# A fused two-layer transformer kernel: paired maxima, DMA-transposed keys, PSUM operands, and another way to round the FFN's integers

## What is computed

```python
# layer 0, cross-attention, 16 heads of 8; ctx has 120 positions
q = rms_norm((x @ Wq + bq) per head, gq);  k = rms_norm((ctx @ Wk + bk) per head, gk)
out = softmax(q k^T / sqrt(8)) @ v;        x = x + out @ Wproj + bproj
# layer 0, FFN with integers: act_quant rounds to -128..127 per row, weight_quant to -1, 0, 1
h = act_quant(ln(x)) @ weight_quant(w1)^T; h = silu(depthwise_conv1d(h, 3 taps))
x = x + act_quant(h) @ weight_quant(w2)^T
# layer 1, cross-attention, one head of 128, keys and values are ctx itself
a = softmax((ln(x) @ w1_w^T + w1_b) ctx^T / sqrt(128)) @ ctx
x = x + concat(ln(x), a) @ w2_w^T + w2_b
# layer 1, mixture of 8 experts of width 256, every row goes to all of them
x = x + sum_e softmax(ln(x) @ gate)_e * ((silu(ln(x) @ Wg_e) * (ln(x) @ Wu_e)) @ Wd_e)
```

## Time and profile before

| | |
|---|---|
| median of the runs | 1234.42 us |
| the profiled execution | 1234.41 us, span 1232.5 us |
| TensorE products busy | 1122.8 us (91%), 10033 records |
| VectorE | 1043.8 us (85%), 2728 |
| ScalarE | 836.8 us (68%), 1685 |
| GpSimd | 695.4 us (56%), 827 |
| mean granted TensorE clock | 0.983 |

### The profile page before, as it was taken

How to read it: one execution, slowest core, us unless ns; L and a number is a source line. 1 busy time by engine, 2 the same in 40 slices (tenths; PEclk the granted TensorE clock), 3 DMA queues, 4 the chain that set the end, 5 groups by cost and what they waited for, 6 DMA issues and landing times.

```text
span 1232.5 us, 27848 instructions
## 1 busy us (share of the span) xinstructions
PE 1122.8 (91%) x10033; PEld 805.9 (65%) x10033; DVE 1043.8 (85%) x2728; ACT 836.8 (68%) x1685; POOL 695.4 (56%) x827
## 2 busy tenths in 40 slices
PE   4498889999999898998899999999989999999998
PEld 3476656666767575665767567576757666767676
DVE  6778897998989899899798989999998988878553
ACT  2144567777877686777678667777867777867655
POOL 3222235557564747567374746748474747476775
PEclk9699999999999999999899999999999999999999
DMA  6222205022312111121302112221211122020100
GB/s 197 53 48 48 63 5 87 4 48 59 73 28 52 30 32 43 44 51 39 59 13 58 31 38 44 54 61 29 54 34 30 24 52 43 1 52 4 40 10 9
DMA packets 151400, 53.67 MB, mean 44 GB/s; under 512 B 116833, under 2 KB 150625, under 8 KB 150881
## 3 DMA queue, kind: packets, MB, share of 16 engines
q1 hardware_dynamic: 149248, 47.82, 18.5%
q10 hardware_dynamic: 2016, 4.08, 0.9%
HBM read 24.73 MB, written 4.19 MB: 23 GB/s over the span
## 4 chain that ended last, share of the span: by engine, by line
PE 57%; DVE 28%; ACT 6%; issue 3%; SPq 2%; POOL 2%; DMA 1%; POOLq 0%; DVEq 0%; ACTq 0%
PE py L783 11%; PE pg L773 3%; PE pa L597 3%; DVE moe L1363 3%; DVE q_st L1202 3%; PE pg L775 3%; PE pg L774 3%; PE pu L773 3%; PE pu L775 3%; PE pu L774 3%; PE pa L633 3%; DVE xn L1251 2%; PE pb L680 2%; ACT probs L849 2%; DVE h L1272 2%
## 5 line engine op out<-in xcount | busy, mean ns | idle before, releaser
L1000 POOL TENSOR_TENSOR moe<-moe 128x512 f32<-128x512 f32 x256 | 329.9, 1292 | 299.4 <-ACT moe L931 179.2
L783 PEld LDWEIGHTS py<-wd_s,moe 128*128 128x128 f32 x1856 | 236.4, 192 | 26.5 <-issue 3.9
L783 PE MATMUL py<-wd_s,moe 128*128 128x128 f32 x1856 | 250.1, 278 | 3.0 <-ACT side L927 1.7
L915 ACT ACTIVATE tg<-pg 128x512 f32<-128x512 f32 x232 | 139.9, 603 | 86.3 <-PE pg L775 84.1
L1202 DVE TENSOR_REDUCE q_st<-pa 128x4 f16<-128x480 f32 x256 | 168.0, 656 | 24.8 <-PE pa L597 23.0
L1363 DVE SCALAR_TENSOR_TENSOR moe<-tg,pg 128x512 f32<-128x512 f32 x232 | 157.5, 679 | 30.4 <-ACT tg L915 28.0
L849 ACT ACTIVATE probs<-pa 120x512 f32<-120x512 f32 x256 | 139.3, 602 | 26.2 <-PE pa L623 25.9
L931 ACT ACTIVATE moe<-pu 128x512 f32<-128x512 f32 x232 | 140.1, 604 | 19.7 <-PE pu L775 16.7
L597 PE MATMUL pa<-kbd,qht 128*128 128x480 f16 x256 | 95.5, 373 | 17.4 <-DVE q_st L1202 13.9
L773 PE MATMUL pg<-x4h,wg_h 128*128 128x512 f16 x232 | 89.3, 385 | 14.2 <-DVE moe L1363 12.7
L955 POOL TENSOR_SCALAR xn<-x,lnm,lnr 128x128 f32<-128x128 f32 x192 | 97.2, 518 | 2.6 <-POOL lnr L950 0.7
(11 more groups left out here) (198 smaller groups left out, 2663.9 us busy)
## 6 DMA issues: line engine op xcount, KB each, us to landing
kbd<-kht SPq DMA_DIRECT2D x512, 3.8 KB
xin<-in_x SPq DMA_DIRECT2D x16, 256.0 KB, 3.1
xres<-in_x SPq DMA_DIRECT2D x16, 256.0 KB, 3.0
out_x<-acc SPq DMA_DIRECT2D x16, 256.0 KB, 2.6
ctxt_a<-in_ctx_t SPq DMA_DIRECT2D x16, 240.0 KB, 3.2
ctxt_b<-in_ctx_t SPq DMA_DIRECT2D x16, 240.0 KB, 3.3
ctxn_b<-in_ctx SPq DMA_DIRECT2D x16, 240.0 KB, 4.1
wd_s<-in_wd ACTq DMA_DIRECT2D x1, 1024.0 KB, 8.8
```

What stands on the lines that cost most here:

```text
L783: mm = pe.matmul(moe_y(g, e)[:, j, :], hu[:, u % 3, j * S:(j + 1) * S], wd_s[:, u, :], start=(half == 0 and j == 0), stop=(half == 1), ski ...
L915: act.activation(tg[:, u % 2, 0:wide], moe_bank("g", g, u)[:, 0:wide], ACT.Tanh, scale=0.5 / WSCALE)\
L1000: pool.tensor_tensor(hu[:, u % 3, 0:wide], gw[:, u % 3, 0:wide], us[:, u % 3, 0:wide], ALU.mult)\
```

## The change

1. Maxima: each product covers 32 rows (four heads) and 480 columns; two, of different rows and into different banks (S0 and BM, which now lie side by side: S1 and S0 change numbers), are read by one VectorE reduce of 960 elements. Two such steps per sequence in place of four.
2. Keys: ScalarE spreads k of each sequence into kx, zeros between, so that one DMA transpose per sequence gives the block-diagonal tile. kht, its transpose, the 32 small DMAs per group and kbd's memset of 7680 elements go; kx is cleared instead (4*4*136).
3. PSUM operands: tanh writes over bank PB, and SiLU reads it there; PB is free for the next block after SiLU (h2_done). The exponentials of stage d are written over their scores, and the normalisation reads them there (S1 is free after it).
4. FFN input: rounding by ScalarE (new step "round"), taking off and scaling back by GpSimd (new step "xq"), four instructions each.
5. FFN integers: ScalarE writes them once, as f16 with 1536 added, which rounds; a product of -1536 with the sum of w2 over its four blocks, ahead of each output's four, takes it off.
6. The output scale inv2 is computed once per group. The products "oc" are replaced by "cw": the context times w2_w's second half, early in stage d, and "fused" multiplies the probabilities with that. The untransposed context isn't loaded any more.
7. All orders are new, and UNREAD: 183 dummy products at 54 places for 166 at 53, the last at step 124 for 158.

The diff, cut to its core (the strings of ORDER, declarations and renamed semaphores are left out):

```diff
-S0, S1, BM, BO, PB = range(5)
+S1, S0, BM, BO, PB = range(5)
...
             def do_m(name, t, c, g):
-                sp.wait_ge(kht_in.sem, kht_in.at(g, 16))
...
+                sp.wait_ge(kx_done.sem, kx_done.at(g, t + 1))
                 if later(g):
-                    sp.wait_ge(max_ps.sem, max_ps.at(g - 1, 4 * size(g - 1)))
-                load_part(g, 1)
+                    sp.wait_ge(max_ps.sem, max_ps.at(g - 1, 2 * min(t + 1, size(g - 1))))
+                sp.dma_start_transpose(kbd[:, t, :, :], kx[:, t, :, :].rearrange("p i x -> p (i x)")[:, 0:HQ * 128])\
+                    .then_inc(kbd_in[t].sem, 16)
...
-                take(BM, max_done, g, 4 * t + c + 1)
-                pe.matmul(pa[:, BM, 0:4 * SC], qht2[:, g % 2, t, :],
-                          kbd[:, t, 4 * c:4 * c + 4, :], start=True, stop=True).then_inc(max_ps.sem, 1)
+                take(S0, max_done, g, 2 * t + c + 1)
+                take(BM, max_done, g, 2 * t + c + 1)
+                for psum, part in ((S0, 2 * c), (BM, 2 * c + 1)):
+                    r = slice(32 * part, 32 * part + 32)
+                    mm = pe.matmul(pa[:, psum, 0:4 * SC], qht2[r, g % 2, t, :], kbd[r, t, :, 0:SC], start=True, stop=True)
+                mm.then_inc(max_ps.sem, 1)
...
-                    take(PB, cv_done, g, t + 1)
+                    take(PB, h2_done, g, t + 1)
...
                     for j in range(size(g)):
+                        pe.matmul(pb[:, j * D:(j + 1) * D], unmagic16[:, :], w2_sum[:, :], start=True, stop=False)
                         for k in range(KB):
                             mm = pe.matmul(pb[:, j * D:(j + 1) * D], hi_t[:, j, k, :], w2_i[:, k, :],
-                                           start=(k == 0), stop=(k == KB - 1))
+                                           start=False, stop=(k == KB - 1))
...
-                elif step == "oc":
+                elif step == "cw":
                     for j in seqs:
-                        mm = pe.matmul(pd[:, j * S:(j + 1) * S], ctxn_b[0:SC, j, :], p1t[0:SC, j * S:(j + 1) * S],
-                                       start=True, stop=True)
-                    mm.then_inc(oc_ps.sem, 1)
+                        mm = pe.matmul(pd[0:SC, j * D:(j + 1) * D], ctxt_b[:, j, :], aw2_s[:, 1, :], start=True, stop=True)
+                    mm.then_inc(cw_ps.sem, 1)
...
+                elif name == "kx":
...
+                    for j in range(n):
+                        act.activation(kx[0:SC, j, :, 0:128].rearrange("p i (c x) -> p c i x", c=HQ)[:, :, :, 0:HD],
+                                       kb[0:SC, j, :].rearrange("p (c i d) -> p c i d", c=HQ, i=HQ), ACT.Copy)\
+                            .then_inc(kx_done.sem, 1)
...
+                if name == "round":
+                    act.wait_ge(sc1_done.sem, sc1_done.at(g))
+                    for j in range(n):
+                        ins = act.activation(xn2[:, j, :], xn2[:, j, :], ACT.Identity, bias=magic[:, 0:1], scale=sc1[:, j:j + 1])
...
-                    act.activation(th[:, t % 2, 0:wide], cv[:, t % 2, 0:n, :], ACT.Tanh, scale=0.5).then_inc(th_done.sem, 1)
+                    act.activation(pb[:, 0:wide].rearrange("p (t s) -> p t s", t=n), cv[:, t % 2, 0:n, :], ACT.Tanh, scale=0.5).then_inc(th_done.sem, 1)
...
-                    act.activation(hr[:, t % 2, :], pb[:, :], ACT.Identity, bias=magic[:, 0:1],
-                                   scale=sc2[:, t:t + 1]).then_inc(hr_done.sem, 1)
...
-                    act.activation(hq[:, t % 2, :], hr[:, t % 2, :], ACT.Identity, bias=unmagic[:, 0:1])\
-                       .then_inc(hq_done.sem, 1)
+                    act.activation(hq[:, t % 2, :], pb[:, :], ACT.Identity, bias=magic16[:, 0:1], scale=sc2[:, t:t + 1])\
+                        .then_inc(hq_done.sem, 1)
...
-                        ins = act.activation(p1[:, j, :], pd[:, j * SC:(j + 1) * SC], ACT.Exp, bias=nmax1[:, j:j + 1],
+                        ins = act.activation(pd[:, j * SC:(j + 1) * SC], pd[:, j * SC:(j + 1) * SC], ACT.Exp, bias=nmax1[:, j:j + 1],
...
-                        pool.memset(kbd[:, :, :, :], 0.0).then_inc(kbd_clear.sem, 1)
+                        pool.memset(kx[:, :, :, :], 0.0).then_inc(kx_clear.sem, 1)
...
+                elif name == "xq":
+                    pool.wait_ge(xr_done.sem, xr_done.at(g))
+                    for j in range(n):
+                        ins = pool.tensor_scalar(xn2[:, j, :], xn2[:, j, :], unmagic[:, 0:1], am1[:, j:j + 1], ALU.add, ALU.mult)
...
                 dve.wait_ge(max_ps.sem, max_ps.at(g, 2 * t + c + 1))
+                dve.tensor_reduce(q_st2[:, g % 2, t, 8 * c:8 * c + 8, 3 * HD].rearrange("p (b h) -> p b h", b=2),
+                                  pa[:, S0:BM + 1, 0:4 * SC].rearrange("p b (h k) -> p b h k", h=4), AX.X, ALU.max,
                                   negate=True).then_inc(max_done.sem, 1)
...
-                    elif t == 2:
-                        cb.mark(dve.reciprocal(sc1[:, 0:n], am1[:, 0:n]))
-                    elif t == 3:
-                        for j in range(n):
-                            ins = dve.tensor_scalar(xn2[:, j, :], xn2[:, j, :], sc1[:, j:j + 1], MAGIC, ALU.mult, ALU.add)
...
+                        dve.reciprocal(sc1[:, 0:n], am1[:, 0:n]).then_inc(sc1_done.sem, 1)
...
-                    dve.scalar_tensor_tensor(out=h2[:, t, 0:wide], in0=th[:, t % 2, 0:wide], scalar=1.0,
+                    dve.scalar_tensor_tensor(out=h2[:, t, 0:wide], in0=pb[:, 0:wide], scalar=1.0,
...
-                    ins = dve.tensor_scalar(inv2[:, t:t + 1], am2[:, t:t + 1], wm2[:, 0:1], None, ALU.mult)
                     if t == n - 1:
-                        cb.mark(ins)
+                        cb.mark(dve.tensor_scalar(inv2[:, 0:n], am2[:, 0:n], wm2[:, 0:1], None, ALU.mult))
```

More of the change, by code:

```diff
@@ L71 @@
+        "dcnbbbbadbbbbcdbdbbbcacc",
     ),
     "pe": (
[L73 to L76 removed]
@@ L276, in build_program @@
         dup_done = signal("dup_done", 2)
-        kht_in, qht_in, ks_in = signal("kht_in", 16), signal("qht_in", 16), signal("ks_in", 16)
-        kbd_in = [[signal(f"kbd{half}{c}_in", 16 * HQ) for c in range(4)] for half in range(2)]
-        max_ps, max_done = signal("max_ps", 0, 4), signal("max_done", 0, 4)
+        qht_in, ks_in = signal("qht_in", 16), signal("ks_in", 16)
+        kbd_in = [signal(f"kbd{t}_in") for t in range(GB)]
+        max_ps, max_done = signal("max_ps", 0, 2), signal("max_done", 0, 2)
         st_ps, st_done = signal("st_ps", 0, 1), signal("st_done", 0, 1)
@@ L331, in size, with arrivals @@
             return SIZES[g]
-        def first_half(g):
-            return SIZES[g] // 2
+        def arrivals(t, g):
+            return 16 * sum(1 for h in range(g + 1) if SIZES[h] > t)
         def nth(e):
@@ L361, in steps_of @@
                 if stage == "m":
-                    return [("max", t, c) for t in seqs for c in range(4)]
+                    return [("max", t, c) for t in seqs for c in range(2)]
                 if stage == "c":
                     return of_units("gu", lambda u: True)
-                return plain({"w": "bvt bw wsum", "n": "xn1t q k v", "d": "xn3t bf s1 p1t oc fused xn4t gate"}[stage])
+                return plain({"w": "bvt bw wsum", "n": "xn1t q k v", "d": "cw xn3t bf s1 p1t fused xn4t gate"}[stage])
             if engine == "act":
@@ L399, in steps_of @@
                 return [("hit", t, 0) for t in seqs]
-            return plain({"w": "", "n": "xin ctxa kht qht ks kbd0", "m": "kbd1", "a": "xres", "d": "ctxb", "c": "out"}[stage])
+            if stage == "m":
+                return [("kbd", t, 0) for t in seqs]
+            return plain({"w": "", "n": "xin ctxa qht ks", "a": "xres", "d": "ctxb", "c": "out"}[stage])
         def run(engine, do, between=None):
```

254 lines of the change are left out of this document (112 added, 142 removed).

## The result

The changed kernel takes 1197.38 us (median of 4 runs, 1196.35 to 1199.95) against 1234.56 us for the kernel before: ratio 0.9704, 95% interval 0.9686 to 0.9722. That is 37 us, where 43 were forecast (1191.2, range 1163 to 1226). The profiled execution took 1196.35 us, with a span of 1194.5. The total is near the forecast one, but none of its terms is: what comes ahead of the first product of stage c and what was to be taken off TensorE gave 20 us less than forecast, and the holes gave 14 more. That the misses cancel is luck.

A forecast was written before the change was run, and what follows sets the result against it. VectorE's pace bounds the fill; from 185 us TensorE's queue sets the time, with 58.5 us of holes. 1234.4 - 3 (opening) - 10 (fill) - 13.2 (TensorE) - 17 (holes) = 1191.2 us, range 1163 to 1226.

The forecast's parts named there:

- VectorE: VectorE's load: 95 us less of 1044, from maxima, FFN input rounding, SiLU at 680 ns with tanh in PSUM, output scale.
- ScalarE and GpSimd: Their load: ScalarE comes out even at 74%; GpSimd gains 33 us, off the path while its queue has slack.
- The pairs: Maximum products on TensorE: two 32-row products side by side take 0.23 us, not 0.40; 97 pairs after 185 us save 17.
- Rival B: Products don't overlap and holes only change their owner: 1225 us; chance 0.17.
- The correcting products: On TensorE, a product ahead of each of 64 FFN outputs, 0.06 us each: +3.8 us.
- The holes: TensorE's four largest waits, all on VectorE, 34.1 us: half given back, 17 us, as VectorE's load falls; bounds 0 and 34.
- rival C: More than the sum: all four TensorE waits and the fill's whole idle time go, 1164 us; chance 0.10.
- The opening: Start of the first group: smaller GpSimd memset lets VectorE back sooner, -3 us; bounds 0 and -4.6.
- The fill proper: 47 to 185 us: fewer maxima and waits, transposes for small key DMAs, less PB's hold: -10 us; bounds -20 and 0.
- The sum behind the fill: After 185 us: -13.2 us net off TensorE's products and -17 us out of its waits.
- far ahead: "cw" in place of "oc" in stage d's attention chain: its only wait, the context, is put far ahead; no size given.

The follow-up runs named there:

- x4: Changed kernel with tanh written to SBUF again and bank PB freed after the convolution: 1202.66 us, ratio 0.9762.
- y1: Changed kernel with ScalarE's two passes over the FFN integers again and no correcting product: 1224.65 us, ratio 0.9934.
- w1: Changed kernel with each pair of 32-row maximum products issued twice into the same two banks: 1216.19 us, ratio 0.9872.
- x1: Changed kernel with each pair of 32-row maximum products made two full-row (128-row) products: 1198.9 us, ratio 0.9725.
- y2: Changed kernel without the 64 correcting products, single pass kept: 1196.64 us, ratio 0.9712.
- b1 to b3: Kernel before, old orders, plus: single pass with correcting product (1234.2 us); FFN input rounding off VectorE (1238.35); both and output scale once per group (1248.27).
- x3: Changed kernel with the rounding of the FFN input back on VectorE, ScalarE's and GpSimd's steps empty: 1240.21 us, ratio 1.0064.
- z1: Changed kernel with group 0's "cw" product and its ScalarE copy moved later in their orders: 1196.72 us, ratio 0.9714.

## Why the forecast held, step by step

The total held because misses cancelled. In the spans, 13 us were forecast ahead of the first product of stage c and 5.0 came, 13.2 off TensorE and 1.5 came, 17 out of the holes and 31.5 came.

- **VectorE.** 95 us less was forecast, 86 came (1044 to 957.8). The reduce and SiLU are right to within 4 ns each. SiLU's size is right, its reason only in part (x4).
- **ScalarE and GpSimd.** Even on ScalarE, as forecast (836.8 us busy before, 833.9 after); GpSimd's 33 us were 27.8, and its wait 0.5 us. y1 shows what was missed: ScalarE's room was needed.
- **The pairs: the step that failed.** "A pair costs one product and about 0.03" is right of two products in a run of 32-row products (w1: 0.20 for the second pair) and wrong of a pair alone: the change of row size costs 0.10 us on either side. Forecast -17 us, measured 0 (x1). The rate of eight scores hid it, since it spreads the border over four pairs. Rival B had the right price for the pairs with the wrong reason: the products do overlap, and their borders cost what the overlap gives. In the rest it was wrong.
- **The correcting products.** +3.8 forecast, and right in price: 0.06 us each in the chain (y2).
- **The holes: mis-sized.** Half of 34.1 us was given back, 17; of the four waits 4.4 us are left (0.5 + 1.6 + 2.3; the convolution's is not in the list), and TensorE's idle time fell by 31.5. That is near rival C's end. The reason given, a less loaded VectorE, is at best half of it: b1 to b3 took load away and nothing, or less than nothing, came of it, while x3 and y1 put load back and lost 40 and 25 us. Load and order work together here: room in an engine's queue turned into time only with an order that asks for its results later or issues them sooner. That reading fits all of these runs; that neither would do without the other is shown for these parts only.
- **The opening and the fill: too much.** 13 us were forecast ahead of the first product of stage c, 5.0 came. The opening went from -3 (its own terms, 7.00 - 2.4 - 0.9, give 3.7) to +1.8, with "cw" in the wrong place; moving it gave 2.2 back (z1). The fill proper then gave 6.8 of its 10. The chain of waits no longer runs through SyncE between 100 and 180 us, where the 32 small DMAs were; one landing of kbd is left in it, 2.51 us at 39.2. In the fill VectorE is busy 79% in place of 86%, and the chain there still runs through its maxima. The 17 more dummy products stand in the same stretch; what they cost was not tried.
- **The sum behind the fill.** -13.2 and -17, forecast -30.2; measured -33.0, made of -31.5 idle and -1.5 busy. Of TensorE's busy time, +4 for the corrections and 0 for the pairs would make it 5.5 more than it is. The forecast left the clock out, and it goes most of the way. Three stretches of the kernel before and one of those after (the other two are at 1.00 as well):

```profile
400.00:500.00 100.00, 91.86 (x883) 63.06 (x880) 91.07 (x239) 71.46 (x146) 63.74 (x78) 0.98 0.14 33
600.00:700.00 100.00, 94.36 (x860) 65.77 (x858) 87.43 (x241) 69.94 (x143) 60.64 (x71) 0.97 0.18 40
700.00:800.00 100.00, 92.72 (x834) 63.57 (x833) 91.86 (x228) 73.10 (x149) 63.57 (x74) 0.98 0.22 45
600.00:700.00 100.00, 99.60 (x919) 70.17 (x918) 86.00 (x228) 77.55 (x167) 68.52 (x90) 1.00 0.26 52
```

Before, TensorE was granted 0.98, 0.97 and 0.98 of its clock in them, and 1.00 in the rest of 185 to 1232 us: 2 + 3 + 2 = 7 us of work at full clock, as an estimate from rounded shares. After, no such stretch is left. The same shows over whole executions, in each of them: 0.980 to 0.989 granted for the kernel before, 0.991 to 0.993 for the changed one. So about 7 of the 33 us are clock (an estimate, beside a busy time that y1 and y2 show to be good to several us only), in stretches where TensorE had been busy 92 to 94% of the time and is busy 98 to 100% now; that fewer holes are the reason fits x3, where the holes and the lower clock came back together, but is not shown by itself, and 900 to 1000 us, 91% busy before, was granted 1.00. How much of the 13 us forecast for the fill the clock changed (0.96 and 0.99 for 47 us on) was not tried.

How much an order made anew would have won with the old work stays open as well; it wasn't tried.

## What to carry to other kernels

Small-row products side by side pay only in a run: count the borders to full-row products (0.10 us each here), and put two pairs or more together before counting a gain. Where every engine's order is fixed, work taken off a busy engine may be worth nothing until the order is made for it (b1 to b3), and work put back can cost as much as it takes or more (x3: 38 us of VectorE, 40 us of time); so read, beside each engine's load, at which place in the order its result is asked for. A step put "far ahead" has to be checked in the first group by itself.

## What the chip did that I had not expected

- A 32-row product and a full-row one next to each other expose the weight load, 0.09 to 0.10 us; between products of full rows it is hidden, and within a run of four 32-row products as well.
- ScalarE's 128x128 rounding from SBUF takes 484 ns on average, its copy of 120x128 304: two operations of nearly the same size, and neither is near the one price of 360 used for both.
- Tanh of 128x512 written to PSUM takes 603 ns, 639 to SBUF before and 630 in x4.
- A sum over 512 f16 elements beside GpSimd's memset took 1.04 us and a cast of 128 elements 1.14, where the line of the maxima gives 0.69 for the first and 0.2 was allowed for the second; both have their operands in SBUF.
